# Value-times-output product of a cross-attention kernel: keys on the output partitions, 26 of 154 tokens in four 32-column float32 tiles ahead of a 128-token main product

## Chip, cores and metric

One core of one Trainium2 chip. The metric is device microseconds (us) of one execution, lower is better.

## What is computed

`x` is 2 x 2048 x 512 (queries), `ctx_768` is 2 x 77 x 384 (keys and values), 8 heads of width 512:

```python
Q = (img_embed @ Wq).reshape(B, -1, H, D).transpose(0, 2, 1, 3)
K = (sent_embed @ Wk).reshape(B, -1, H, D).transpose(0, 2, 1, 3)
V = (sent_embed @ Wv).reshape(B, -1, H, D).transpose(0, 2, 1, 3)
score = jnp.einsum('bhqd,bhkd->bhqk', Q, K) / math.sqrt(D)
attn = softmax(where(mask, score, -inf))
ctx = jnp.einsum('bhqk,bhkd->bqhd', attn, V).reshape(B, -1, H * D)
out = ctx @ Wo + img_embed
return (out - mean) * rsqrt(var + 1e-5) * gamma + beta
```

Everything is float32. The two products with the queries are reassociated: A = Wq K^T and VW = V Wo are made per head from the 154 tokens (2 batches x 77 keys), so that the queries meet only A (scores) and VW (output).

## The kernel before

**Two stages.** The first is a loop over 16 uses `u` (8 key heads, then 8 value heads, `H` = 8). The second goes over 32 tiles of 128 queries, in 16 pairs `p`: seven block products with A (a Strassen-like scheme), softmax, a transpose of the probabilities, and the product with VW, then the layer norm.

**Numbers in two parts.** Most products are made of float32r parts: a rounded `hi` and a remainder `lo`, three terms out of four. `short_product` (L538) takes hi weights against a moving operand that holds hi and lo side by side (304 or 308 columns), and lo weights against hi alone (152 or 154). `full_product` (L546) multiplies plain float32; each float32 matmul of the code is two records of 154 columns in the trace.

**A use u.** TensorE (PE) makes `project(u+1)` or `project_full(u+1)` (tokens times Wk or Wv, 12 matmuls of the code), and then the out product of `u` (16 matmuls of the code: `out_product` or `out_product_full`). Weights stand still, so the tokens are the columns of the result and the model dimension is on its partitions. ACT rounds the weights (`round_w_proj` L828, `round_w_out` L836), the projected values (`round_kv` L846), and takes the out product (L853). GpSimd (POOL) makes the `lo` part of the projection weights (L1489), VectorE (DVE) the `lo` part of the out weights (`split_w_out`, L1061), of the projected values (`split_kv`, L1080 to L1089) and of A (L1105 to L1113). Which value heads go in parts and which in plain float32 is set by hand (`SPLIT_VALUES`, `FULL_VALUES`): projections of 8, 9, 13, 14, 15 and out products of 8, 12, 13, 14 are in parts.

**VW.** The out product of a value head lies as model x tokens in `vw_t`. The second stage wants keys on the partitions, so `transpose_vw` (L651) turns blocks of 128 rows over TensorE inside the out products of uses 10, 12, 13, 15 and once more in `first_products(0)`: 40 transposes of 128 columns. ACT (L861) and DVE (L1130) split each into `vw_hi` and `vw_lo`: 10 instructions of 512 columns each.

**The T sums.** During uses 8 to 10 DVE also makes the sums that the block scheme needs: `right_sum` (L1159, 16 instructions of 608 columns, both inputs in SBUF), `split_t` (L1164, 8 of 608 columns); ACT rounds them (`round_t`, L900). They read all of A, so they start after the last key head.

**Order.** Each engine runs its own list in program order; semaphores connect them. In use 8 and later DVE has, in this order: `split_kv(u+1)` (or `add_kv`), `split_vw`, and behind them the T sums of that use. `project_full(u+1)` starts by waiting for what DVE or ACT made of the projection of `u` (`wait_kv(u)`), because it overwrites the same PSUM banks. The DMA queue of SyncE (SP) loads weights in rings of three, then the query blocks.

**Start of the second stage.** `bias_rows` (L1144) waits for the out product of use 14, ACT's `seed(0)` (L871) waits for it, `first_products(0)` waits for the seed. In DVE's list `split_vw(H, [0])` stands between `add_u2(0)` (L1177) and `add_w2(0)` (L1182), and the product S4 in `last_products(0)` waits for `add_w2(0)`. `normalise` (L1243, L1246) scales 616 probabilities by the reciprocal of their sums before `transpose_prob` (L724); `out_rows` (L737) is 15 matmuls of 512 columns.

Of the kernel before, what the change touches and what calls it, by code (L numbers as in the profile page):

```python
# [26 lines left out]
F32 = mybir.dt.float32  # L27
F32R = mybir.dt.float32r
# [10 lines left out]
PAD_FROM = 96  # L39


class Shapes:


    def __init__(self, x_tiles, ctx_t, w_proj, w_out, mask):
# [15 lines left out]
        self.slot = self.keys + self.keys % 2  # L61
        self.key_t = -(-self.row // P)
        self.per_batch = self.tiles // self.batches
        assert self.toks == self.batches * self.keys and self.half <= BANK and self.heads % 2 == 0
        assert 2 * self.toks <= BANK and self.model <= BANK and self.dim_t == self.model_t == 4
        assert self.batches == 2 and self.kept % 2 == 0 and self.heads // 2 * self.slot <= BANK

    def key_rows(self, j):
        return min(P, self.row - j * P)


def transposes_during(s):


    plan, j = [], 0
    for h in range(s.heads + 1):
        ready = []
        while j < s.key_t and j * P + s.key_rows(j) <= s.keys * h:
            ready += [(j, b) for b in range(s.batches)]
            j += 1  # L80
        plan.append(ready)
    return plan


def build(nc, x_tiles, x_rows, ctx_t, wk, wq_t, wv, wo, mask, gamma, beta, out):
# [8 lines left out]
    SPLIT_VALUES = (H, *range(H + 4, USES - 1))  # L94
    FULL_VALUES = (H + 2, H + 3, H + 4)
# [10 lines left out]
    plan = transposes_during(s)  # L106
    groups = [g for part in plan for g in part]
    group_no = {g: n for n, g in enumerate(groups)}

    with ExitStack() as stack:  # L110
# [47 lines left out]
        with ExitStack() as values:  # L158
            v_t0 = values.enter_context(nc.sbuf_tensor("v_t0", [P, s.dim_t, s.toks], F32))
            values.enter_context(nc.sbuf_tensor("gap6", [P, s.dim_t, s.toks], F32))  # L160
            v_t = [v_t0, values.enter_context(nc.sbuf_tensor("v_t1", [P, s.dim_t, s.toks], F32))]
# [4 lines left out]
        with ExitStack() as spare:  # L166
            t_tmp4 = [spare.enter_context(nc.sbuf_tensor(f"t_tmp4_{n}", [P, KT, s.kept_half], F32)) for n in range(3)]
# [5 lines left out]
        w_proj_hi = []  # L173

        def vw_and_proj(name, n):

            with ExitStack() as early:
                early.enter_context(nc.sbuf_tensor(f"vw_first{n}", [P, FREE_VW, s.batches, s.model], F32R))
                w_proj_hi.append(early.enter_context(nc.sbuf_tensor(f"w_proj_hi{n}", [P, s.dim_t, s.ctx_t, P], F32R)))
            return sb(name, [P, s.key_t, s.batches, s.model], F32R)  # L180
# [18 lines left out]
        sb("gap2", [P, 288])  # L199
# [1367 lines left out]
```

## Time and profile before

| | us |
|---|---|
| median of 3 runs | 352.82 (352.49 to 353.0) |
| the profiled execution, its own time | 353.7 |
| its span in the profile | 351.9 |
| PE busy | 346.0 (98%), 2272 matmuls |
| DVE busy | 288.0 (82%) |
| ACT busy | 243.7 (69%) |
| POOL busy | 213.3 (61%) |
| PE clock granted | 9 tenths or more in every one of 40 slices |

The profiled execution's time is its span and 1.8 us around it. A busy share counts time in which an instruction of the engine is under way; matmuls overlap, so the start of one to the start of the next is what one costs.

### The profile page before, as it was taken

To read this page: it belongs to the slowest core of one execution; us is meant where nothing else is said; L and a number is where in the kernel's file an instruction comes from. 1 tells how busy PE (TensorE), PEld (TensorE's weight loads), DVE (VectorE), ACT (ScalarE), POOL (GpSimd) and SP (SyncE) were. 2 spreads that over 40 slices of the span, in tenths; PEclk is the share of its full clock that TensorE was granted. 3 is DMA by queue.
4 is the path that set the end of the run, shared out by engine and by line. 5 is a ranking of instruction groups with operands and counts; after the bars stand their busy time and mean duration, and the time that the engine had idled before them with its cause. 6 is when DMAs were issued, how large, how long until landed. Compare 5 with 4: busy or idle time off the path is not lost. (4 is left out here: it accounts for less than half of the span.)

```text
span 351.9 us, 6894 instructions
## 1 busy us (share of the span) xinstructions
PE 346.0 (98%) x2272; PEld 322.0 (92%) x2272; DVE 288.0 (82%) x532; ACT 243.7 (69%) x797; POOL 213.3 (61%) x218
## 2 busy tenths in 40 slices
PE   9999999999999999999999999999999999999994
PEld 6999999999999999998899899889988998899884
DVE  2149999999778768898797988988987989889896
ACT  2268766645777669887886976968778769768560
POOL 0044654400447968689769688687796796885243
PEclk9999999999999999999999999999999999999999
DMA  7998769775635080053142341440532423413012
GB/s 229 423 420 323 280 223 324 281 276 218 221 137 212 0 275 29 1 179 113 68 171 75 116 151 59 152 151 31 181 95 85 152 72 138 149 41 111 32 44 107
DMA packets 19683, 55.81 MB, mean 159 GB/s; under 512 B 1728, under 2 KB 3264, under 8 KB 17728
## 3 DMA queue, kind: packets, MB, share of 16 engines
q1 hardware_dynamic: 18784, 54.38, 42.6%
q10 hardware_dynamic: 864, 1.00, 0.8%
q8 instruction: 18, 0.29, 0.4%
q14 instruction: 17, 0.14, 0.1%
HBM read 46.98 MB, written 8.39 MB: 157 GB/s over the span
## 5 line engine op out<-in xcount | busy, mean ns | idle before, releaser
L1489 POOL TENSOR_TENSOR w_proj_lo<-w_proj,w_proj_hi 128x768 fp32r<-128x768 f32 x20 | 36.9, 1868 | 73.1 <-ACT w_proj_hi L828 73.1
L737 PE MATMUL pair<-vw_hi,pt_hi 128*128 128x512 f32 x155 | 62.1, 400 | 0.0
L737 PE MATMUL pair<-vw_lo,pt_hi 128*128 128x512 f32 x155 | 60.9, 393 | 0.0
L737 PE MATMUL pair<-vw_hi,pt_lo 128*128 128x512 f32 x155 | 60.7, 392 | 0.0
L1438 POOL TENSOR_TENSOR out_sb<-centred,beta_sb 128x512 f32<-128x512 f32 x30 | 38.8, 1295 | 28.8 <-ACT centred L939 28.7
L894 ACT ACTIVATE prob<-c,neg_max 128x77 f32<-128x77 f32 x128 | 43.9, 347 | 0.0
L1483 POOL TENSOR_TENSOR xo_lo<-x_sum,xo_hi 128x512 fp32r<-128x512 f32 x32 | 41.5, 1301 | 0.2 <-ACT xo_hi L918 0.2
L538 PE MATMUL pair<-kv_t,w_out_hi 128*128 128x304 f32 (+1 forms) x160 | 41.6, 334 | 0.0
L661 PE MATMUL pair<-a_hi,xo_hi 128*128 128x304 f32 x128 | 40.0, 313 | 0.0
L661 PE MATMUL pair<-a_lo,xo_hi 128*128 128x304 f32 x128 | 38.6, 302 | 0.0
L661 PE MATMUL pair<-a_hi,xo_lo 128*128 128x304 f32 x128 | 38.6, 301 | 0.0
L1262 DVE TENSOR_TENSOR pair<-pair,x_in 128x512 f32<-128x512 f32 x31 | 21.7, 699 | 19.5 <-PE pair L737 19.3
L932 ACT ACTIVATE pt_hi<-pair 128x640 fp32r<-128x640 f32 x32 | 22.5, 704 | 21.4 <-PE pair L724 21.4
L1061 DVE TENSOR_TENSOR w_out_lo<-w_out,w_out_hi 128x1024 fp32r<-128x1024 f32 x20 | 33.1, 1692 | 3.8 <-ACT w_out_hi L836 3.7
L885 ACT ACTIVATE prob<-pair,neg_max 128x77 f32<-128x77 f32 x64 | 19.9, 325 | 23.0 <-DVE neg_max L1205 23.0
L737 PEld LDWEIGHTS pair<-vw_hi,pt_lo 128*128 128x128 f32 x155 | 29.2, 188 | 6.3
L737 PEld LDWEIGHTS pair<-vw_hi,pt_hi 128*128 128x128 f32 x155 | 29.2, 188 | 5.4
L737 PEld LDWEIGHTS pair<-vw_lo,pt_hi 128*128 128x128 f32 x155 | 29.2, 188 | 5.0
L1477 POOL TENSOR_TENSOR xo_lo<-xt_in,xo_hi 128x512 fp32r<-128x512 f32 (+1 forms) x32 | 33.2, 1038 | 0.9 <-ACT xo_hi L911 0.9
L1432 POOL TENSOR_TENSOR rstd<-var_eps,minus_half 128x1 f32<-128x1 f32 x32 | 17.7, 553 | 25.5 <-DVE var_eps L1283 25.5
L538 PE MATMUL pair<-kv_t,w_out_lo 128*128 128x152 f32 (+1 forms) x160 | 32.5, 244 | 0.0
L661 PE MATMUL pair<-t_hi,xo_hi 128*128 128x304 f32 x96 | 29.5, 307 | 0.2 <-DVE c L1201 0.2
(129 smaller groups left out, 1022.3 us busy)
## 6 DMA issues: line engine op xcount, KB each, us to landing
w_out<-wo SPq DMA_DIRECT2D x8, 1024.0 KB, 4.8
xt_in<-x_tiles SPq DMA_DIRECT2D x16, 512.0 KB, 4.0
x_in<-x_rows SPq DMA_DIRECT2D x16, 512.0 KB, 4.7
out<-out_sb SPq DMA_DIRECT2D x31, 256.0 KB, 2.1
w_out<-wq_t SPq DMA_DIRECT2D x7, 1024.0 KB, 8.1
w_proj<-wv SPq DMA_DIRECT2D x8, 768.0 KB, 4.7
w_proj<-wk SPq DMA_DIRECT2D x6, 768.0 KB, 9.9
w_out<-wq_t SPq DMA_DIRECT2D x2, 512.0 KB, 8.2
```

Of the source, the lines that this page charges most:

```text
L538: mm = pe.matmul(pair[:, bank, 0:n], w[:, m, k, :], moving[:, k, 0:n], start=(at == 0), stop=(at == len(steps) - 1))
L661: mm = pe.matmul(bank, xs[:, left, k, :], kept_heads(r[:, k, :]), start=(begin and k == 0 and n == 0), stop=(k == KT - 1 and n == len(pass ...
L737: mm = pe.matmul(ps_out[:, i % 2, 0:s.model], ps[:, j, :], v[:, j, b, :], start=(j == 0 and n == 0), stop=(j == s.key_t - 1 and n == len(p ...
L885: e = act.activation(prob[i % 2][:, h * s.keys:(h + 1) * s.keys], src, ACT.Exp, bias=neg_max[i % 2][:, h:h + 1], accum_out=sums[i % 2][:, ...
L894: e = act.activation(prob[i % 2][:, cols], c2[:, cols], ACT.Exp, bias=neg_max[i % 2][:, h:h + 1], accum_out=sums[i % 2][:, h:h + 1])
L932: act.activation(pt_hi[i % 2][:, :, :], pt_blocks, ACT.Copy).then_inc(act_pt_hi, 1)
L1061: dve.tensor_tensor(half_cols(w_out_lo[u % W_RING], half), half_cols(w_out_sb[u % W_RING], half), half_cols(w_out_hi[u % 2], half).bitcast ...
L1262: dve.tensor_tensor(y, ps_out[:, i % 2, 0:s.model], x_in[c % X_RING][:, i % CHUNK, :], ALU.add)\
L1438: pool.tensor_tensor(out_sb[i % OUT_RING][:, :], centred[i % 2][:, :], beta_sb[:, :], ALU.add)\
L1477: pool.tensor_tensor(xo_lo[p % 2][:, blocks, :, :], src, xo_hi[p % 2][:, blocks, :, :].bitcast(F32), ALU.subtract).then_inc(pool_xo_lo, 1)
L1483: pool.tensor_tensor(xo_lo[p % 2][:, blocks, :, :], x_sum[:, at:at + 2, :, :], xo_hi[p % 2][:, blocks, :, :].bitcast(F32), ALU.subtract).t ...
L1489: pool.tensor_tensor(half_cols(w_proj_lo[u % W_RING], half), half_cols(w_proj_sb[u % W_RING], half), half_cols(w_proj_hi[u % 2], half).bit ...
```

## The change

VW is made with the tokens on the output partitions: the projected values stand still, the rows of Wo move (512 columns). Of the 154 tokens, 128 in the middle (the last 64 keys of one batch and the first 64 of the other) are the main product in three float32r passes, 12 matmuls of 512 columns. The 26 others (13 at each end) are padded to 32 (`v_rest`) and multiplied in plain float32, in four column tiles of the array, one for each 128 columns of Wo: 16 matmuls of the code with 128 moving columns. They write 32 partitions each; ACT copies them to `strip_sb`, and SP moves each in 8 small DMAs to `rest_rows`, from which the fifth block of VW is split at the start of the second stage. Odd heads take the tokens with the batches exchanged (`ctx_turned`). The transposes and `vw_t` go. All value heads are projected in plain float32, all out products are in parts; the `lo` weights of uses 8 to 13 are made by POOL, those of 14 and 15 by DVE. `normalise` writes the 13 end keys of each head to `prob_rest` with an instruction of its own.

```diff
-    SPLIT_VALUES = (H, *range(H + 4, USES - 1))
-    FULL_VALUES = (H + 2, H + 3, H + 4)
+    RESTS_OF_VECTOR = (USES - 2, USES - 1)
+    STRIPS = P // STRIP
...
         def whole(u):
-            return u < FULL_PROJ or u in FULL_VALUES
+            return u < FULL_PROJ or u >= H
         def whole_out(u):
-            return u < FULL_OUT or (u >= H and u not in SPLIT_VALUES)
+            return u < FULL_OUT
+        def by_vector(u):
+            return u < H or u in RESTS_OF_VECTOR
...
+            def move_strips(h):
+                sp.wait_ge(act_strip, h + 1)
+                for g in range(STRIPS):
+                    for n in range(s.batches):
+                        b = (h + n) % 2
+                        to, at = place(h, b) * s.rest, g * STRIP + n * s.rest
+                        sp.dma_start(rest_rows[to:to + s.rest, b, g * P:(g + 1) * P],
+                                     strip_sb[h % 2][at:at + s.rest, :]).then_inc(ld_rest[h % 2], DMA_INC)
...
                 load_w_out(u)
+                if u >= H + W_RING:
+                    move_strips(u - H - W_RING)
             for c in range(XT_RING):
                 load_xt(c)
+            for h in range(H - W_RING, H):
+                move_strips(h)
...
+            def value_product(u):
+                h = u - H
+                hi, lo = wide(w_out_hi[u % 2]), wide(values_lo(u))
+                wait_kv(u, 1)
+                if u == USES - 1:
+                    open_bank_a()
+                if h == 0:
+                    pe.wait_ge(dve_a_lo, 2 * H)
+                elif h >= 2:
+                    pe.wait_ge(dve_vw_lo, 2 * (h - 1))
+                for k in range(s.dim_t):
+                    if k % 2 == 0:
+                        pe.wait_ge(act_o_hi, 2 * split_before(u) + k // 2 + 1)
+                        pe.wait_ge(dve_o_lo if by_vector(u) else pool_o_lo,
+                                   rests_before(u, by_vector(u)) + k // 2 + 1)
+                    passes = [(0, hi), (0, lo), (1, hi)]
+                    for n, (low, w) in enumerate(passes):
+                        mm = pe.matmul(ps_vw[h % 2], values(u, k, low), w[:, k, :], start=(k == 0 and n == 0),
+                                       stop=(k == s.dim_t - 1 and n == len(passes) - 1))
+                mm.then_inc(pe_outp, 1)
+            def value_strips(u):
+                h, w = u - H, wide(w_out_sb[u % W_RING])
+                pe.wait_ge(pool_v_rest, h + 1)
...
+                for k in range(s.dim_t):
+                    for g in range(STRIPS):
+                        mm = pe.matmul(ps_strips[h % 2][g * STRIP:(g + 1) * STRIP, :], v_rest[u % 2][:, k, :],
+                                       w[:, k, g * P:(g + 1) * P], start=(k == 0), stop=(k == s.dim_t - 1))
+                mm.then_inc(pe_outp, 1)
...
                 if whole_out(u):
                     out_product_full(u)
+                elif u < H:
+                    out_product(u)
                 else:
-                    out_product(u)
+                    value_strips(u)
+                    value_product(u)
...
+            def take_strips(h):
+                act.wait_ge(pe_outp, 2 * (H + h) + 1)
...
+                act.activation(strip_sb[h % 2][:, :], ps_strips[h % 2], ACT.Copy).then_inc(act_strip, 1)
+            def split_rest():
+                for n in range(2):
+                    act.wait_ge(ld_rest[n], DMA_INC * STRIPS * s.batches * (H // 2))
...
             for u in range(USES):
+                if u + 1 < USES and u >= H:
+                    round_w_out(u + 1)
                 if u + 1 < USES:
                     round_kv(u + 1)
...
                 if u == USES - 1:
                     seed(0)
-                if u >= H:
-                    split_vw(u - H)
...
+                take_strips(u - H)
+                split_vw(u - H)
...
             copy_s1(0)
             round_sums(1)
-            split_vw(H)
+            split_rest()
             exps_first(0)
...
                 if u + 1 < USES and not whole_out(u + 1):
                     split_kv(u + 1)
-                elif u + 1 < USES and summed_kv(u + 1):
-                    add_kv(u + 1)
                 if u == H:
                     right_sum(T1, 0)
...
+                if u + 1 < USES and by_vector(u + 1):
+                    split_w_out(u + 1)
...
             add_u2(0)
-            split_vw(H, [0])
+            split_rest(0)
             add_w2(0)
...
+            for u in range(H, USES):
+                if not by_vector(u):
+                    for half in range(2):
+                        pool.wait_ge(act_o_hi, 2 * split_before(u) + half + 1)
+                        pool.tensor_tensor(half_cols(values_lo(u), half), half_cols(w_out_sb[u % W_RING], half),
+                                           half_cols(w_out_hi[u % 2], half).bitcast(F32), ALU.subtract)\
+                            .then_inc(pool_o_lo, 1)
+                pool.wait_ge(dve_kv_lo, 2 * split_before(u) + 2)
...
+                pool.tensor_tensor(v_rest[u % 2][:, :, 0:s.rest_toks].rearrange("p m (n k) -> p m n k", n=2),
+                                   rest_values(u, 0), rest_values(u, 1), ALU.add)\
+                    .then_inc(pool_v_rest, 1)
+                if u == USES - 2:
+                    block_sums(0)
```

`values(u, k, low)` is the 128 tokens from column 13 on of `kv_t[u % 2]`, its hi or its lo part; `wide(w)` is a row block of Wo as 512 columns. `ctx_turned` is copied by POOL at the start of the kernel, while POOL has nothing else.

## Rows read from the trace of the kernel before

**Rows 1.** Busy time in stretches (us, then PE, PEld, DVE, ACT, POOL, clock, DMA).

```profile
65.48:68.52 3.04, 3.04 (x26) 3.04 (x26) 3.04 (x2) 1.24 (x3) 1.11 (x1) 1.00 0.54 175
68.52:72.55 4.03, 4.03 (x34) 4.03 (x33) 3.93 (x8) 0.86 (x2) 0.00 (x0) 1.00 0.84 324
72.55:75.69 3.14, 3.14 (x25) 3.14 (x25) 3.07 (x6) 0.86 (x2) 0.00 (x0) 1.00 0.54 179
75.69:79.89 4.20, 4.20 (x34) 4.20 (x33) 4.03 (x6) 2.85 (x5) 0.00 (x0) 1.00 0.81 309
98.50:103.40 4.90, 4.90 (x41) 4.90 (x41) 2.88 (x8) 3.58 (x7) 3.46 (x2) 1.00 0.26 109
140.00:340.00 200.00, 199.80 (x1182) 180.11 (x1181) 172.56 (x350) 153.76 (x609) 147.62 (x163) 1.00 0.29 104
```

**Rows 2.** Timeline of PE (start us, us): output product, stage two's start, its S4, kernel's start.

```profile
151.54 0.39 PE L737 MATMUL pair<-vw_hi,pt_hi 128*128 128x512 f32 x1
151.77 0.39 PE L737 MATMUL pair<-vw_lo,pt_hi 128*128 128x512 f32 x1
...
123.52 0.41 PE L661 MATMUL pair<-a_hi,xo_hi 128*128 128x304 f32 x1
...
128.68 0.30 PE L661 MATMUL pair<-a_hi,xo_hi 128*128 128x304 f32 x1
...
0.77 3.57 PE L759 MATMUL pair<-const-bfloat16-1.0 128*128 128x512 bf16 x8 [0.77 <-PEq L1560]
```

**Rows 3.** POOL by tile (duration ns min/median/max) and its timeline at use 13.

```profile
L1489 POOL TENSOR_TENSOR w_proj_lo<-w_proj,w_proj_hi x20: 1818/1861/2062, 21.0 to 109.7; 128x768 fp32r<-128x768 f32 x20
...
L1483 POOL TENSOR_TENSOR xo_lo<-x_sum,xo_hi x4: 1276/1282/1289, 117.6 to 126.9; 128x512 fp32r<-128x512 f32 x4
...
92.70 3.64 POOL L1489 TENSOR_TENSOR w_proj_lo<-w_proj,w_proj_hi 128x768 fp32r<-128x768 f32 x2 [26.11 <-ACT w_proj_hi L828]
```

**Rows 4.** Timeline and tiles where DVE and POOL both read two SBUF tensors.

```profile
57.68 1.86 POOL L1489 TENSOR_TENSOR w_proj_lo<-w_proj,w_proj_hi 128x768 fp32r<-128x768 f32 x1
58.19 2.44 DVE L1061 TENSOR_TENSOR w_out_lo<-w_out,w_out_hi 128x1024 fp32r<-128x1024 f32 x1
...
112.17 1.23 DVE L1061 TENSOR_TENSOR w_out_lo<-w_out,w_out_hi 128x1024 fp32r<-128x1024 f32 x1 [0.15 <-ACT w_out_hi L836]
112.33 1.69 POOL L1460 TENSOR_TENSOR x_sum<-x_sum,xt_in 128x256 f32<-128x256 f32 x1
113.31 1.78 DVE L1061 TENSOR_TENSOR w_out_lo<-w_out,w_out_hi 128x1024 fp32r<-128x1024 f32 x1
...
L1460 POOL TENSOR_TENSOR x_sum<-x_sum,xt_in x2: 734/1210/1685, 112.3 to 122.1; 128x256 f32<-128x256 f32 x2
```

**Rows 5.** Timeline of DVE, T sums and their remainders.

```profile
78.55 2.44 DVE L1159 TENSOR_TENSOR t_tmp<-t_tmp,t_tmp 128x608 f32<-128x608 f32 x3
...
83.72 1.49 DVE L1164 TENSOR_TENSOR a_lo<-t_tmp,a_hi 128x608 fp32r<-128x608 f32 x2
```

**Rows 6.** Timeline of ACT, rounding of out weights and of VW.

```profile
63.98 2.00 ACT L836 ACTIVATE w_out_hi<-w_out 128x1024 fp32r<-128x1024 f32 x2
...
122.34 1.08 ACT L861 ACTIVATE vw_hi<-pair 128x512 fp32r<-128x512 f32 x2 [0.41 <-PE pair L651]
```

**Rows 7.** Timelines of DVE and SP around the second stage's start; DMA issues (KB, us to landing).

```profile
119.55 1.85 DVE L1144 TENSOR_TENSOR mask_bias<-mask_low 128x308 f32<-128x308 f32 x2
...
126.64 0.69 DVE L1130 TENSOR_TENSOR vw_lo<-pair,vw_hi 104x512 fp32r<-104x512 f32 x1 [0.67 <-ACT vw_hi L861]
127.25 0.46 DVE L1182 TENSOR_TENSOR u_w<-pair,u_w 128x304 f32<-128x304 f32 x1
...
123.82 1.39 SPq L467 DMA_DIRECT2D x_in<-x_rows  x3
...
out<-out_sb SPq DMA_DIRECT2D x1, 128.0 KB, 1.7
```

**Rows 8.** DVE by tile: scaling of the probabilities (duration ns min/median/max).

```profile
L1246 DVE TENSOR_TENSOR prob<-prob,pair x32: 795/796/797, 132.7 to 337.5; 128x616 f32<-128x616 f32 x32
```

More of the change, by code:

```diff
@@ L39 @@
 PAD_FROM = 96
+STRIP = 32
 class Shapes:
@@ L61, in __init__ @@
         self.slot = self.keys + self.keys % 2
+        self.main = P // self.batches
+        self.rest = self.keys - self.main
+        self.rest_toks = self.batches * self.rest
+        self.rest_rows = self.heads * self.rest
         self.key_t = -(-self.row // P)
@@ L65, in __init__ @@
         assert 2 * self.toks <= BANK and self.model <= BANK and self.dim_t == self.model_t == 4
+        assert 0 < self.rest_toks <= STRIP and self.rest_rows <= P and self.heads * self.main == (self.key_t - 1) * P
         assert self.batches == 2 and self.kept % 2 == 0 and self.heads // 2 * self.slot <= BANK
[L68 to L82, printed above, removed]
 def build(nc, x_tiles, x_rows, ctx_t, wk, wq_t, wv, wo, mask, gamma, beta, out):
@@ L340, in head_cols @@
         def head_cols(t, half, h):
-            keys = s.kept if t is a_hi or t is a_lo else s.keys
-            return t[:, 2 * half:2 * half + 2, :, h * keys:(h + 1) * keys]
+            rows = t[:, 2 * half:2 * half + 2, :, h * s.kept:(h + 1) * s.kept]
+            apart = s.kept_row + (place(h, 1) - h) * s.kept
+            return bass.AP(rows.tensor, rows.offset, [*rows.ap[0:2], [apart, s.batches], rows.ap[-1]])
         def tile_cols(w, m):
@@ L384, in split_before, with rests_before, values, ends_of @@
             return sum(not whole_out(v) for v in range(u))
-        def summed_before(u):
-            return 2 * sum(not whole_out(v) for v in range(H, u))
-        def value_of(u):
-            return kv_full[u] if u < FULL_OUT else v_t[u % 2][:, :, :]
+        def rests_before(u, of_vector):
+            return 2 * sum(not whole_out(v) and by_vector(v) == of_vector for v in range(u))
+        def by_vector(u):
+            return u < H or u in RESTS_OF_VECTOR
+        def values(u, k, low):
+            at = low * s.toks + s.rest
+            return kv_t[u % 2][:, k, at:at + P]
+        def ends_of(rows, count):
+            return bass.AP(rows.tensor, rows.offset,
+                           [*rows.ap[:-1], [2 * s.keys, count], [2 * s.keys - s.rest, 2], [1, s.rest]])
+        def rest_values(u, low):
+            return ends_of(kv_t[u % 2][:, :, low * s.toks:(low + 1) * s.toks], 1)[:, :, 0, :, :].bitcast(F32)
+        def mains_of(t):
+            return t.rearrange("p (j k) -> p j k", k=2 * s.keys)[:, :, s.rest:s.rest + P]
+        def place(h, b):
+            return h ^ b
+        def values_lo(u):
+            return wo_lo_even if (u - H) % 2 == 0 else wo_lo_odd[1] if u < H + 5 else wo_lo_late
+        def vw_half(v, h, n):
+            return v[n * s.main:(n + 1) * s.main, h // 2, (n + h) % 2, :]
+        def wide(w):
+            return w[:, :, :, :].rearrange("p k m c -> p k (m c)")
         def nth_product(p, n):
```

243 lines of the change are left out of this document (105 added, 138 removed).

## The prediction

> **What bounds the kernel now.** I read the table of stretches first. In each stretch of the value heads PE is busy for all of it, at full clock, and from 140 to 340 us it works 199.80 of 200 us [rows 1]. The view of waits names PE for nothing but the 0.77 us at the very start [rows 2]. So PE bounds both stages, and each microsecond added to its list or put as a gap into it is lost. DVE is busy 172.56 of 200 us in the second stage [rows 1]. In the value heads it is nearly as full as PE (3.93 of 4.03 us, 3.07 of 3.14), while POOL is empty there: before 92.70 it sat idle for 26.11 us [rows 3]. The second view is the timeline where DVE and POOL work together. A DVE subtraction of 1024 columns from two SBUF tensors takes 1.23 us alone, but 2.44 us when it begins at 58.19, with a POOL instruction under way until 57.68 + 1.86 = 59.54: 59.54 + 1.2 is when it ended. The other way round, POOL's 0.73 us sum began at 112.33 and took 1.69, for it had to let the DVE instruction of 112.17 end; and the next one of DVE (1.78) waited for that [rows 4]. So where both engines read two SBUF tensors they go one at a time, a whole instruction each, in turn.
>
> **PE's own work, use 8 to the end of 15.** Removed: four out products in parts at 4.03 and four plain ones at 4.20, 32.9 us, and 32 transposes of four calls at 4.90 - 4.03 = 0.87 each, 3.5 us (the fifth call is after the end of use 15) [rows 1]. Together 36.4. Added: per head a main product of 12 matmuls of 512 columns, which start 151.77 - 151.54 = 0.23 us apart [rows 2], so 2.74 us; and the strips. Projections: five go from 3.04 to 3.14 [rows 1], +0.5.
>
> The strips are the first unknown. A plain projection is 24 records of 154 columns in 3.14 us, 0.131 us each [rows 1]; at 128 columns that is 0.109. A head has 16 strip matmuls, 32 records. If nothing overlaps that is 3.5 us; if four tiles run at once, 0.9. The two records of one matmul need the same columns of the array one after the other, and the neighbour's first can only run beside the second of them if starts keep their order. That is half of the serial price, and between the two ends: I take 2.0 us with a little for starts. Then a head costs 4.74 and eight cost 37.9: PE's work grows by 37.9 - 36.4 + 0.5 = 2.0 us.
>
> The Trainium skill (TensorE: Matmul & The Clock Gate, Part 3, packing of small matmuls) measured 2.38 times the speed for three column tiles; carried over to four that would make a head's strips about 1.1 us (an estimate), and PE's work would shrink by 5 us instead. It speaks of matmuls of one pass, and no run here shows column tiles.
>
> **Gap 1, before the strips of use 8: 1.7 us.** The strips wait for `v_rest`, which stands in POOL's list behind both halves of `w_out_lo(8)`. ACT rounds those at 63.98 and gives the first free at 65.0 [rows 6]. POOL's price for 1024 columns isn't in the trace: 768 take 1.86, 512 take 1.28 [rows 3], so 2.4. Two halves from 65.1 end at 69.9, the small sum at 70.4 (0.45, an estimate below the 0.73 of 256 columns [rows 4]). PE has done the projection of 9 at 68.7. Lower bound 0 (if POOL could start at the landing), upper 2.5.
>
> **Gap 2, before the projection of 11: 7.7 us.** Before, the projected values of 10 needed ACT alone; now `project_full(11)` waits for DVE's `split_kv(10)`, which stands behind nine T sums. PE: strips from 70.5, product of 8 done at 75.2, projection of 10 78.4, strips 80.4, product of 9 83.1; here it wants `kv(10)`. DVE: `split_vw(0)` can start at 75.9 (ACT 0.5 [rows 6]), but in front of it T1's three sums alternate with POOL's `w_out_lo(9)` (70.4 on), so it ends at 79.4. Then nine sums at 2.44 / 3 = 0.81 [rows 5], 7.4 us, and between them POOL's two halves of `w_out_lo(10)`, of which 3.6 us fall into this piece, since DVE and POOL take turns [rows 4]. 79.4 + 11.0 + 0.4 = 90.8. Without the turns it would be about 1.9 us.
>
> **Gap 3, before the projection of 12: 5.0 us.** PE needs 3.15 + 2.0 + 2.74 = 7.9 us for the next three pieces. DVE needs from 90.8: the other half of `kv(10)` 0.4, two splits of VW 1.2, six `split_t` at 0.72 [rows 5] 4.3, POOL's two halves of `w_out_lo(11)` between them 4.8, two sums 1.6, `kv(11)` 0.4: 12.8. Without POOL's turns 8.0, a gap of 0.1. Then PE does the projection, strips and product of 11 by 111.6, and four heads with three projections, 4 x 4.74 + 3 x 3.15 = 28.4, end at 140.0 against 123.52 [rows 2]. That is 16.5 later. In these last heads ACT has some 4.5 us and POOL 5.3 to do in 7.9: no gap.
>
> **Gap 4, before S4 of the first pair: net 3.4 us.** Before, S4 began 5.16 us after use 15's end [rows 2]. Now a chain of small DMAs is ahead of it. `bias_rows` (1.85 [rows 7], and two turns of POOL, 1.5) waits for the product of 14, which now ends only 4.7 us before the end; the seed follows at +0.7 to +1.1 and holds ACT's `take_strips(7)`; SP issues eight DMAs at 1.39 / 3 = 0.46 or somewhat less [rows 7], to +4.9; the last lands 1.7 to 2 later, by the smallest DMA of the trace [rows 7], +6.8; ACT 0.5, DVE 0.6, `add_w2` 0.4 [rows 7]: S4 at +8.5. Bounds: 0 if the DMAs are issued and land in half that, 5 if they meet others. Behind it the fifth transposition call is gone, already counted in the 5.16.
>
> **At nothing.** `normalise` pays 0.80 us for 616 columns [rows 8]; 512 and 104 apart cost perhaps 0.15 more, 32 times on DVE, which has 27 of 200 us idle [rows 1], and PE reads the result some 4 us later. Cover gone, it would be 4.8 us in all, at worst. The five pairs of weight roundings that go from ACT, the four out-weight subtractions that go from DVE, and the early copies on POOL lie beside PE's work. SP's 64 small DMAs take 3.4 us per head in a queue where a load is issued about one head ahead of its use; bounds 0 and 2 us.
>
> **Clock.** All stretches show full clock [rows 1]; but the first eight matmuls after nothing took 3.57 / 8 = 0.45 us for 512 columns instead of 0.23 [rows 2], the 1.2 GHz level. Gaps of 5 to 8 us could bring that back. The price of one restart from these rows is 1.7 us; gaps 3 and 4 could each leave one, so 0 to 3.4, and I take 1.4.
>
> The Trainium skill (TensorE: Matmul & The Clock Gate, Part 1) says that an idle array falls back to half its clock; no gap of this trace is long enough to show it.
>
> **Sum.** 2.0 + 1.7 + 7.7 + 5.0 + 3.4 + 1.4 = 21.2 us. The profiled execution took 353.7 (span 351.9 and 1.8), so it would show 374.9, a span of 373.1; the median of the runs is 0.9 lower, so 374.0.
>
> **The rivals.**
> *Turns harmless (0.17).* POOL's work falls where DVE uses PSUM inputs or waits. Gaps 2 and 3 are 1.9 and 0.1, the sum 2.0 + 1.7 + 2.0 + 3.4 = 9.1: 362; with strips at 1.1 us, 7 less from PE but some back in the gaps, about 356. For it: splits with a PSUM input aren't slowed. Against: T sums are SBUF only and fill DVE's list here.
> *Strips serial (0.12).* 3.5 us, eight times 1.5 more, of which gaps 2 and 3 take back 6: 380. For it: every record has its own weight load, and in the trace a load goes with each matmul.
> *Faster: four tiles at once (0.13).* One mechanism, at the strips: 0.9 us per head. PE's work falls by 36.4 - 29.1 - 0.5 = 6.8 us, and the fifth transposition call (0.8) with it; if the four gaps together stay under 7.6 us the kernel is faster, and with none of them it is 352.8 - 7.6 = 345.2. It decides from 1.75 us per head on. Against it: each gap is a wait in program order and is longer when PE arrives sooner.
> *No difference (0.03)*, where these cancel within 0.2%, about 0.7 us, which is what a measurement of this kernel can tell from nothing.
> The forecast has 0.55. That the change doesn't do what it says (tiles placed apart) is the serial case.
>
> **Numbers.** 374.0. With serial strips and a restart 381, without turns 356: these two ends leave out the faster cases and little else. Slower: 0.55 + 0.17 + 0.12 = 0.84.
>
> **What would show it.** Right: PE idle before the first record of the projections of uses 11 and 12, put down to DVE `kv_t`; DVE's T sums taking 2 to 3.2 us each when POOL's 1024-column instruction is under way; PE idle before the first strips (POOL `v_rest`) and before S4; the second stage as long as before. Wrong: strips of about 1 us and PE without idle time in the value heads, or T sums that stay at 0.8 us beside POOL. If 16 strip matmuls take other than 2.0 us, the first term fails and the rest stands.

## The result, and the profile after

The changed kernel takes 374.90 us (median of 4 runs, 373.82 to 375.72), the kernel before on the same chip 352.91 (4 runs, 352.49 to 353.11): a ratio of 1.0623 with a 95% interval of 1.059 to 1.0656, 22.0 us slower. The profiled execution below took 375.72 with a span of 373.9, which is 22.0 more than the span before.

The page of the kernel after: the span, the busy time of each engine, and of the 40 slices of the span the busy tenths of PE and DVE and the clock granted to PE.

```profile
span 373.9 us, 7129 instructions
PE 346.6 (93%) x2328; PEld 313.7 (84%) x2328; DVE 295.3 (79%) x557; ACT 245.0 (66%) x794; POOL 231.1 (62%) x232
PE   8999999793699963999999999999999999999994
DVE  2269997679972782789898898889888889889896
PEclk9999999896999997899999999999999999999998
```

PE is busy for 346.6 us, the same to 1 us as before, but 93% of the span instead of nearly all of it. The lost time is in slices 8 to 16, from 70 to 150 us. The next view is PE's timeline there: start, duration, line, operation, number of records, and in brackets the idle time ahead of it and what ended it. The rows without brackets show one undisturbed head.

```profile
70.56 1.85 PE L693 MATMUL pair<-w_out,v_rest 128*32 128x128 f32 x32 [1.97 <-POOL v_rest L1539]
90.48 5.40 PE L586 MATMUL pair<-ctx_turned,w_proj 128*128 128x154 f32 x24 [7.11 <-DVE kv_t L1126]
102.90 3.38 PE L586 MATMUL pair<-ctx_sb,w_proj 128*128 128x154 f32 x24 [3.02 <-DVE kv_t L1126]
113.39 1.08 PE L693 MATMUL pair<-w_out,v_rest 128*32 128x128 f32 x32
117.29 3.31 PE L586 MATMUL pair<-ctx_sb,w_proj 128*128 128x154 f32 x24
120.53 1.08 PE L693 MATMUL pair<-w_out,v_rest 128*32 128x128 f32 x32
133.34 1.08 PE L693 MATMUL pair<-w_out,v_rest 128*32 128x128 f32 x32 [1.61 <-POOL v_rest L1539]
139.20 0.38 PE L703 MATMUL pair<-a_hi,xo_hi 128*128 128x304 f32 x1 [1.76 <-ACT pair L921]
149.30 0.62 PE L703 MATMUL pair<-a_hi,xo_hi 128*128 128x304 f32 x1 [5.72 <-DVE u_w L1216]
```

Before, PE was busy in all of each stretch of the value heads [rows 1]. Now there are six gaps, 21.2 us in all: before the strips of use 8, before the projections of uses 11 and 12, before the strips of 15, before the first pair's product behind the seed, and before its S4. A head that nothing holds takes 7.14 us (113.39 to 120.53): 1.01 for the strips, 2.89 for the main product, 3.24 for the projection.

Why `kv_t` came late is seen where DVE's T sums (L1193) meet POOL's low weights (L1533). DVE and POOL, timeline:

```profile
71.19 2.83 DVE L1193 TENSOR_TENSOR t_tmp<-t_tmp,a_lo 128x608 f32<-128x608 f32 x1
78.29 0.79 DVE L1193 TENSOR_TENSOR t_tmp<-a_hi,a_lo 128x608 f32<-128x608 f32 x1
79.12 2.87 DVE L1193 TENSOR_TENSOR t_tmp<-t_tmp,a_hi 128x608 f32<-128x608 f32 x1
82.02 2.85 DVE L1193 TENSOR_TENSOR t_tmp<-t_tmp,a_lo 128x608 f32<-128x608 f32 x1
78.60 5.62 POOL L1533 TENSOR_TENSOR wo_lo_even<-w_out,w_out_hi 128x1024 fp32r<-128x1024 f32 x2 [1.97 <-ACT w_out_hi L874]
107.87 4.73 POOL L1533 TENSOR_TENSOR wo_lo_even<-w_out,w_out_hi 128x1024 fp32r<-128x1024 f32 x2 [4.27 <-ACT w_out_hi L874]
```

A T sum is 0.79 us. Each one that meets POOL's pair of 1024 columns is 2.8 to 2.9, 2.0 to 2.1 longer: it waits out nearly a whole POOL instruction (4.73 / 2 = 2.37 undisturbed). POOL's pair grows from 4.73 to 5.62, by about one T sum. These are the turns of [rows 4], with larger instructions. The two held sums at 79 and 82 us are 4.1 of the 7.11 us of the gap before the projection of 11; the other 3.0 are DVE's own list in front of `kv_t` (an estimate, from these rows). The sum held at 71.19 cost nothing, since DVE then waited 2.83 us for ACT, until 76.85.

The tail, from the timelines of SP's queue, ACT and DVE:

```profile
76.60 6.45 SPq L527 DMA_DIRECT2D rest_rows<-strip_sb  x8
117.48 0.34 SPq L519 DMA_DIRECT2D w_out<-wo  x1
117.87 6.69 SPq L527 DMA_DIRECT2D rest_rows<-strip_sb  x8
124.69 0.94 SPq L488 DMA_DIRECT2D xt_in<-x_tiles  x2
125.69 20.65 SPq L527 DMA_DIRECT2D rest_rows<-strip_sb  x24
147.51 1.15 ACT L911 ACTIVATE vw_hi<-rest_rows 104x512 fp32r<-104x512 f32 x2 [5.72 <-DMA rest_rows<-strip_sb]
148.17 0.69 DVE L1163 TENSOR_TENSOR vw_lo<-rest_rows,vw_hi 104x512 fp32r<-104x512 f32 x1 [6.57 <-ACT vw_hi L911]
```

One small DMA keeps SP's queue for 0.8 us (6.45 / 8), and the last 24, which the kernel puts behind the loads of x transposed (`xt_in`), stand one behind the other until 146.34. ACT waits 5.72 us for the last of them, DVE 6.57 for ACT, PE's S4 5.72 for DVE.

Last, stretches of the kernel after: length, busy time and number of instructions of PE, PEld, DVE, ACT and POOL, then PE's granted clock, DMA share and GB/s.

```profile
70.50:76.10 5.60, 5.54 (x45) 4.44 (x46) 3.49 (x2) 0.28 (x1) 5.60 (x3) 0.70 0.26 103
90.40:95.90 5.50, 5.42 (x28) 5.29 (x32) 5.44 (x6) 3.43 (x5) 3.75 (x3) 0.62 0.04 9
102.80:106.30 3.50, 3.40 (x28) 3.27 (x32) 3.40 (x6) 0.35 (x2) 0.38 (x1) 1.00 0.42 161
113.30:120.50 7.20, 7.20 (x70) 6.25 (x68) 2.24 (x4) 4.27 (x8) 4.66 (x3) 1.00 0.45 155
149.30:152.30 3.00, 3.00 (x12) 3.00 (x13) 1.81 (x6) 1.76 (x9) 0.00 (x0) 0.50 1.04 375
```

Behind the gaps of 1.97, 7.11 and 5.72 us the granted clock is 0.70, 0.62 and 0.50 on average, which is wholly or partly the level of 1.2 GHz; behind that of 3.02 it is 1.00.

### The profile page after: what moved, and what is told of

The parts are those of the page before. It is cut to its first block and busy times, and to the rows that moved or that the text cites. A ratio compares the mean times of both kernels' runs of the same rounds, so it can differ in the third digit from the quotient of the medians.

```text
span 373.9 us, 7129 instructions
## 1 busy us (share of the span) xinstructions
PE 346.6 (93%) x2328; PEld 313.7 (84%) x2328; DVE 295.3 (79%) x557; ACT 245.0 (66%) x794; POOL 231.1 (62%) x232
## 5 line engine op out<-in xcount | busy, mean ns | idle before, releaser
L1526 POOL TENSOR_TENSOR w_proj_lo<-w_proj,w_proj_hi 128x768 fp32r<-128x768 f32 x10 | 18.4, 1862 | 28.3 <-ACT w_proj_hi L866 28.3
L703 PEld LDWEIGHTS pair<-a_hi,xo_hi 128*128 128x128 f32 x128 | 24.5, 191 | 8.7 <-DVE u_w L1216 6.0
L703 PE MATMUL pair<-t_lo,xo_hi 128*128 128x304 f32 x96 | 29.3, 305 | 0.0
L703 PE MATMUL pair<-t_hi,xo_lo 128*128 128x304 f32 x96 | 29.2, 305 | 0.0
```

Of the source, the lines that this page charges most:

```text
L703: mm = pe.matmul(bank, xs[:, left, k, :], kept_heads(r[:, k, :]), start=(begin and k == 0 and n == 0), stop=(k == KT - 1 and n == len(pass ...
L1526: pool.tensor_tensor(half_cols(w_proj_lo[u % W_RING], half), half_cols(w_proj_sb[u % W_RING], half), half_cols(w_proj_hi[u % 2], half).bit ...
```

## The experiments

The theory: DVE and POOL take turns where both read two SBUF tensors, and that makes `kv_t` of uses 10 and 11 late; a second, separate delay comes from the strips' small DMAs in the tail. Rivals: DVE has too much to do even without turns; the strips on PE are what costs. Each run below is beside runs of the kernel before on the same chip.

### Low weights on DVE alone

```diff
-    RESTS_OF_VECTOR = (USES - 2, USES - 1)
+    RESTS_OF_VECTOR = range(H, USES)
```

> All eight value heads' low weights are made by DVE instead of POOL for six of them; nothing else changes. Theory (DVE and POOL take turns on two-input SBUF instructions): DVE gets 2.3 us more per head, but none of its T sums is held, all take 0.8 us; the gap before the strips of use 8 goes, the one before the projection of 11 falls from 7.1 to about 4, that of 12 stays near 3, and the kernel gains 5 to 7 us, to about 369. Rival (only the order of DVE's list makes the gaps, turns cost nothing): DVE's list in front of split_kv(10) and (11) grows by 2.3 us each, the gaps grow, 375 or more.

371.76 us, ratio 1.0538 (1.052 to 1.0556). PE's timeline of this kernel before the projection of 11:

```profile
83.25 6.17 PE L586 MATMUL pair<-ctx_turned,w_proj 128*128 128x154 f32 x24 [3.94 <-DVE kv_t L1126]
```

And DVE's T sums, those that took 2.87 and 2.85 us in the changed kernel:

```profile
76.02 0.79 DVE L1193 TENSOR_TENSOR t_tmp<-t_tmp,a_hi 128x608 f32<-128x608 f32 x1
76.84 0.79 DVE L1193 TENSOR_TENSOR t_tmp<-t_tmp,a_lo 128x608 f32<-128x608 f32 x1
```

The gap is 3.94 instead of 7.11, though DVE has four more pieces of 1.23 to make before it, two of them behind its first T sums. The gap before the strips of use 8 is gone. The gap before 12 fell from 3.02 to 0.38, and a new one of 2.00 stands before 13, where DVE is now too full. So the turns were real, and giving the work to DVE trades them for load. The gap of 3.94 us was followed by the slow clock (0.54 over the 6.2 us): the projection took 6.10 us from its start to the next piece, where it took 5.33 in the changed kernel and takes 3.24 undisturbed.

### Strips tile by tile

```diff
-                for k in range(s.dim_t):
-                    for g in range(STRIPS):
+                for g in range(STRIPS):
+                    for k in range(s.dim_t):
```

> The two loops of the strips are exchanged, so that the four matmuls of one column tile follow each other before the next tile. Theory (a strip costs 1.0 us because neighbours in the list are on different tiles and run together): consecutive records meet the same columns, strips go to about 3.5 us per head, 20 us more for eight, of which the two gaps in the T sums take back about 5: about 390. Rival (0.03 us per record is what an instruction costs to issue, whatever tile it has): strips stay at 1.0 us and the time at 375.

382.30 us, ratio 1.081 (1.078 to 1.0839). Two records from its PE timeline:

```profile
123.13 3.31 PE L586 MATMUL pair<-ctx_sb,w_proj 128*128 128x154 f32 x24
126.37 2.46 PE L693 MATMUL pair<-w_out,v_rest 128*32 128x128 f32 x32
```

From the start of one projection to the start of the next are 8.51 us (131.64 - 123.13), less 3.24 and 2.89: 2.4 for the strips, against 1.0 when neighbours in the list are of different tiles. Not the serial 3.5 either. Eight heads times 1.38 are 11.0 us. The gaps before projections 11 and 12 (5.76 and 2.17 here), before the strips of 15 (none), at the seed (0.21) and before S4 (4.78) took back 6.3, and the slow clock, by what is then left, took 1.9 more than in the changed kernel (the projection of 12 in 5.05 instead of 3.38, the first strips 4.05, the projection of 11 4.85). That makes 6.6; the spans differ by 6.5 (380.4 and 373.9). The strips' price in the changed kernel, 1.0 us, is thereby settled, and so is that it is low because neighbours in the list are of different tiles: the rival, 0.03 us as the price of an issue whatever the tile, would have left the time at 375.

### The tail's order and the early `v_rest`

The rows' rounding on ACT and DVE moved behind the first probabilities, the first loads of x transposed issued at use 14, `v_rest(8)` ahead of POOL's low weights of 8.

```diff
+                if u == USES - 2:
+                    for c in range(XT_RING):
+                        load_xt(c)
...
-            split_rest()
             exps_first(0)
             copy_s1(1)
             exps_second(0)
+            split_rest()
```

> Three moves: ACT's and DVE's split of rest_rows goes behind the first softmax, the two loads of query blocks go ahead of the strips' small DMAs of uses 11 and later, and POOL takes v_rest(8) ahead of its low weights of use 8. Theory (these lists hold PE): the 5.7 us gap before S4 and the slow clock behind it (1.4) go, the 1.6 us one before the strips of use 15 and the 2.0 before those of use 8 go with its slow clock (1.6); about 364. Rival (another wait stands behind each: the small DMAs' landing itself, or DVE's list): at most 3 us are won, 372 or more.

372.56 us, ratio 1.0539 (1.0512 to 1.0567), a miss: 2.3 us gained where 11 were expected, as the rival had it. The gaps before the strips of 8 and 15 and before S4 are gone, but the time went elsewhere: 0.62 before the strips of 9, the one before projection 11 grew to 8.19, the seed's to 2.43, and 4.0 us appeared in the main loop (1.91 behind `vw_lo`, 0.91, 1.21). For the 1.91 us behind `vw_lo` PE waited for the same late rows, further down its list. Before projection 11 DVE's T sums were held as before, four of them to 1.88 to 2.88 us each.

### A quarter of the low weights

```diff
+                        part = slice(0, 1) if u in (H + 2, H + 3) else slice(0, s.model_t)
```

with `[:, :, part, :]` on POOL's three operands. It leaves out three quarters of the low parts of `wo` for uses 10 and 11.

> POOL makes only a quarter of the low weights of uses 10 and 11 (256 columns instead of 1024 in each of four instructions); the other three quarters are left out, so these two heads use stale low weights. DVE's list and its work are untouched. Theory (turns): the DVE sums held by POOL take 1.5 us each instead of 2.9, the gap before the projection of 11 falls from 7.1 to about 3.8, that of 12 from 3.0 to about 0, in all 6 us: 369. Rival (order alone): no change, 375.

369.97 us, ratio 1.0461 (1.0417 to 1.0506). PE and DVE of this kernel:

```profile
85.01 5.05 PE L586 MATMUL pair<-ctx_turned,w_proj 128*128 128x154 f32 x24 [3.81 <-DVE kv_t L1126]
76.94 1.21 DVE L1193 TENSOR_TENSOR t_tmp<-t_tmp,a_hi 128x608 f32<-128x608 f32 x1
78.18 1.22 DVE L1193 TENSOR_TENSOR t_tmp<-t_tmp,a_lo 128x608 f32<-128x608 f32 x1
```

The same two T sums that took 2.87 and 2.85 take 1.21 and 1.22 when POOL's instruction has a quarter of the columns. What they wait beyond their own 0.79 us falls from 2.07 to 0.42, as POOL's instruction falls from 1024 to 256 columns, which is what turns of whole instructions mean. The gap before projection 11 falls by 3.30, as much as the two sums are shorter (3.29); 3.81 are left, nearly all of it DVE's own list. The gap before projection 12 is gone, the others unchanged. The profiled execution took 367.31 us and is 2.7 below the median; the clock accounts for part of that, as the last section shows.

### Three heads in plain float32

Uses 9 to 11: `v_t` as a float32 copy, the main product from `w_out_sb` and `v_t` in four float32 matmuls of 512 columns, no roundings and no low weights.

```diff
+                if u in PLAIN:
+                    for k in range(s.dim_t):
+                        at = plain_values(u)[:, k, s.rest:s.rest + P]
+                        mm = pe.matmul(ps_vw[h % 2], at, wide(w_out_sb[u % W_RING])[:, k, :], start=(k == 0),
+                                       stop=(k == s.dim_t - 1))
+                    mm.then_inc(pe_outp, 1)
+                    return
```

> Uses 9, 10 and 11 (value heads 1 to 3) are made in plain float32: no high and low parts of their weights or values, four float32 matmuls of 512 columns per head for the main product, and v_rest copied instead of summed. The four passes of float32 over 512 columns should take 3.6 us where the twelve products take 2.89 (2.1 us more in three heads). Theory of the turns (POOL's low weights against DVE's T sums and kv_t): the gaps of 7.11 us before the projection of use 11 and 3.02 before that of 12 vanish, and with them the slow projection behind the first (5.33 instead of 3.24): 374.9 - 7.1 - 3.0 - 2.1 + 2.1 = 365 us, range 362 to 368. The gap of 1.97 before the strips of use 8 and those of the tail (1.6, 1.8, 5.7) stay. Rival (the T sums and splits of DVE are too much work even undisturbed, so that kv_t comes late without any turn): a gap of 3 to 4 us stays before the projection of 11 and the time is 369 or more. Rival (values without their low parts change nothing, since the release comes from elsewhere): 375.

366.79 us, ratio 1.0383 (1.0349 to 1.0418). PE's timeline:

```profile
85.24 1.08 PE L709 MATMUL pair<-w_out,v_rest 128*32 128x128 f32 x32
86.25 3.70 PE L683 MATMUL pair<-w_out,v_t 128*128 128x512 f32 x8
98.13 2.07 PE L595 MATMUL pair<-ctx_turned,w_proj 128*128 128x154 f32 x14 [0.39 <-DVE kv_t L1142]
```

The gaps before the projections of 11 and 12 are gone, and so is the slow clock behind the first; a new one of 0.39 us stands before that of 13 (the last row); the plain product costs 3.54 (86.25 to the projection at 89.79), 0.65 more than the twelve. The time is 8.1 us below the changed kernel, within the range told. The gaps at both ends stay: 2.50 before the strips of 8 and 2.23 before those of 15, both a little longer, 1.75 and 5.71 around S4.

### The same with the tail mended

As above, with `v_rest(8)` first, the early loads of x transposed, `mask_bias` made at use 12 in the memory of the T sums, and the rows split batch by batch.

```diff
-                if u == USES - 1:
+                if u == H + 4:
                     bias_rows()
...
             split_pt(0)
+            split_rest([0])
...
+                    if j == s.key_t - 1 and i % s.per_batch == 0:
+                        pe.wait_ge(dve_vw_lo, 2 * H + b + 1)
```

> As e4_plain, and with the tail mended as well: POOL makes v_rest(8) before the low weights of use 9; the first load of x transposed is issued at use 14, ahead of the strips' small DMAs; bias rows are made at use 12 in the memory of the T sums instead of at use 15; the strips' rows are split batch by batch, the first after the transposed probabilities of tile 0, the second after those of tile 1. If the gaps found at both ends (1.97 before the strips of 8; 1.61, 1.76 and 5.72 around S4, 1.4 of slow clock behind it) come from those causes, and the two groups (turns, tail) add up: 365 - 2.0 - 0.8 - 9 - 1.4 = 352 us, range 349 to 358, level with the kernel before at 353. Rival (the waits of the tail only move, as in e3_tail, where 4 us of the gaps came back inside the main loop): 357 to 361.

360.73 us, ratio 1.0209 (1.017 to 1.0248). No gap over 0.3 us but 0.39 up to the main loop, and then 6.2 us in it. SP and ACT of this kernel:

```profile
104.72 26.68 SPq L538 DMA_DIRECT2D rest_rows<-strip_sb  x32
131.45 1.55 SPq L505 DMA_DIRECT2D x_in<-x_rows  x3
133.11 0.93 SPq L499 DMA_DIRECT2D xt_in<-x_tiles  x2
139.87 0.63 ACT L981 ACTIVATE xo_hi<-xt_in 128x512 fp32r<-128x512 f32 x1 [5.55 <-DMA xt_in<-x_tiles]
```

The rival had it right: 32 strip DMAs in a row hold the queue until 131.4, the loads of x come behind them, and the tail's wait has moved to x. 6.1 us came off where 13 were expected.

### And with the low weights on DVE

`RESTS_OF_VECTOR = range(H, USES)` on top of it.

> As e6_plain_tail, with the low weights of uses 12 and 13 (and of 8) made by DVE instead of POOL, so that POOL and DVE hold one another nowhere in the value heads. DVE has 4 x 1.23 us more to do in two heads of 7.1. If the turns still cost something in uses 12 and 13: 1 to 2 us below e6_plain_tail. If DVE is then too full, a gap before the projection of 13 or 14 of 2 us and 1 to 3 us above it. My forecast: within 1.5 us of e6_plain_tail.

358.50 us, ratio 1.0155 (1.014 to 1.017): 2.2 below the last, a little beyond the forecast. With three heads plain, DVE has the room that it lacked in the first experiment. But nothing came off the value heads: from the strips of 8 to those of 15 PE needs 49.4 us in both kernels (68.27 to 117.69 and 67.88 to 117.28). 0.9 of the 2.2 us is a shorter wait for x in the main loop (5.25 instead of 6.18), where SP's row of 32 strip DMAs takes 25.61 us instead of 26.68; why it does is not shown.

### All heads plain

`PLAIN = range(H + 1, USES)` on top of the mended tail.

> As e6_plain_tail, with all of uses 9 to 15 in plain float32: no low weights behind use 8, so no turns at all, and ACT and DVE with some 20 us less work each. PE pays 0.7 us per head in four more heads: 352 + 2.8 = 355 us if e6_plain_tail has no gaps left in uses 12 to 15; level with it or faster if it has over 3 us of gaps there. Rival (the float32 product costs no more than the twelve, as both read the same columns): 350.

359.75 us, ratio 1.0191 (1.0152 to 1.023). No wait over 0.5 us up to the main loop, and the same wait for x (6.4 us, before a product of the second pair) stands in it. So by then neither DVE nor POOL nor the turns set the time: SP's queue does.

### The loads of x ahead of the last strips, and two plain heads instead of three

```diff
-            for h in range(H - W_RING, H):
+            for h in range(H - W_RING, H - 1):
                 move_strips(h)
             sp.wait_ge(pe_outp, 2 * USES)
             for c in range(X_RING):
                 load_x(c)
+            move_strips(H - 1)
```

> As e7_plain_tail_dve (358.5 us), with SP issuing the three loads of x rows ahead of the last head's eight strip DMAs instead of behind them. In e7_plain_tail_dve the strips' issues keep SP from 104.8 to 129.6 us; the x rows go out at 129.62, the third load of x transposed at 131.41, and ACT waits 4.63 us for it until 138.54, behind which PE stands idle 5.2 us. Theory (the small DMAs' issues on SP delay the loads, and the load of x transposed is slow because the x rows go out just ahead of it): the load still goes out at 131.4 but lands by 134, the wait of PE falls from 5.2 to 1 us or less, and the time is 354 to 355 us. Rival (the load takes 7 us whatever is beside it, or the strips' last DMAs become what PE waits for): 358 or more.

356.63 us, ratio 1.0101 (1.0086 to 1.0116), the nearest to the kernel before, and between forecast and rival. PE's idle time there:

```profile
141.79 0.41 PE L723 MATMUL pair<-a_hi,xo_hi 128*128 128x304 f32 x1 [2.79 <-ACT pair L942]
```

2.79 instead of 5.2, not under 1: the load of x transposed was issued at 133.10, later than thought, since the eight issues are only shifted. It was there 3.3 us later, at 136.38, and not 7.1 us as behind the x rows; that part of the theory held. Behind the wait the clock fell once more:

```profile
143.07 0.46 PE L723 MATMUL pair<-t_hi,xo_hi 128*128 128x304 f32 x1
```

From 142.31 to 145.60 such products start 0.25 us apart instead of 0.14, which costs some 1.5 us.

> As e9_x_first, with two value heads (uses 9 and 10) in plain float32 instead of three. Each plain head costs PE about 0.7 us; but in use 11 DVE then has the low weights (2.5 us) and the second half of kv_t (0.95) to do again beside the splits of T4. If DVE has that slack: 0.7 us faster than e9_x_first. If not: a gap of 1 to 3 us before the projection of use 12 or 13, and as much slower. My forecast: 1 us slower.

`PLAIN = (H + 1, H + 2)` gave 360.58 us, ratio 1.0214 (1.0191 to 1.0237). Slower by 4 us, not by 1: waits of 1.92 before projection 12 and 1.99 before that of 13, both for DVE's `kv_t`.

```profile
90.15 3.38 PE L599 MATMUL pair<-ctx_sb,w_proj 128*128 128x154 f32 x24 [1.92 <-DVE kv_t L1148]
```

DVE's slack in these heads is under one head's low weights.

### Half of the last strips issued by ACT

Base: the kernel with the low weights on DVE.

```diff
-                for g in range(STRIPS):
+                for g in range(STRIPS if h < H - W_RING else STRIPS // 2):
...
+            def move_half(h):
+                act.wait_ge(act_strip, h + 1)
+                for g in range(STRIPS // 2, STRIPS):
+                    for n in range(s.batches):
...
+                        act.dma_start(rest_rows[to:to + s.rest, b, g * P:(g + 1) * P],
```

> As e7_plain_tail_dve (358.5 us), with half of the strip DMAs of the last three heads issued by ACT instead of SP, so that SP has 12 issues of 0.8 us fewer in front of the loads of x. Theory (SP's issues are the bound of the tail): x rows go out at about 122 us, as soon as the last main product is done, the third load of x transposed when its buffer is free, 129; the wait of PE in the second pair goes: 353 to 354 us, level with the kernel before or faster than e9_x_first. Rival (an issue costs ACT the same 0.8 us, and ACT's splits of the weights and copies of the head then come late): 358 to 362.

357.48 us, ratio 1.0132 (1.0114 to 1.0151). ACT's queue and ACT itself:

```profile
120.46 2.51 ACTq L932 DMA_DIRECT2D rest_rows<-strip_sb  x3
123.06 0.63 ACT L990 ACTIVATE xo_hi<-xt_in 128x512 fp32r<-128x512 f32 x1 [2.37 <-issue]
```

An issue costs ACT the same 0.8 us, and ACT does nothing else meanwhile (2.37 us of "issue"). PE's wait for x (5.25) is gone: the load goes out 1.8 us earlier, and PE comes later, by new waits for ACT (0.99, 1.07) and POOL (1.82) in its timeline. The median is 1.0 us better than without, the intervals of the two ratios overlap, and the time lies between forecast and rival: the price is mostly moved.

### Strips ahead of the out weights' load

```diff
+                if u >= H + W_RING:
+                    move_strips(u - H - W_RING, range(0, 2))
                 load_w_out(u)
...
-                    move_strips(u - H - W_RING)
+                    move_strips(u - H - W_RING, range(2, STRIPS))
```

> As e9_x_first (356.6 us), with the first four of each head's eight strip DMAs issued ahead of the load of out weights of the same turn, which waits for the end of that head's main product, 2.9 us behind the strips. SP, which issues without a pause from 104.7 to 133 us in e9_x_first, then starts that row some 2.9 us earlier. Theory (SP's time for issues is what the loads of x wait for): x rows go out at 122 to 123 instead of 125.1, the third load of x transposed at 130 instead of 133.1, the wait of PE in the second pair falls from 2.8 to under 1 us, and the time is 353.8 to 355 us. Rival (the load's landing or something else sets it): 356 or more. A load of out weights that now goes out late would show as PE idle before a main product and cost 1 to 2 us.

357.85 us, ratio 1.0116 (1.0096 to 1.0137), a miss; no better than the kernel with the loads first, as the rival had it. SP's queue:

```profile
109.35 0.35 SPq L530 DMA_DIRECT2D w_out<-wo  x1
109.76 15.75 SPq L538 DMA_DIRECT2D rest_rows<-strip_sb  x20
125.55 1.54 SPq L505 DMA_DIRECT2D x_in<-x_rows  x3
```

The last load of out weights slipped from 104.15 to 109.35, and the x rows still went out at 125.5. A head's eight issues (6.3 us) and two loads (0.5 each) are 7.3 us on SP, and a head is 7.1 to 7.8 us on PE: the queue is full, and an order can't make room in it. This is what the two misses of the tail have in common.

## Why the prediction was right, and where it wasn't

The forecast was 374.0 and 374.9 came; the sum of the six terms was 21.2, and 22.0 was lost. But this agreement is luck: it is made of errors that cancel. Against their terms PE's own work came out 5.6 us lower, gap 1 0.3 higher, gap 2 0.6 and gap 3 2.0 lower, a gap in no term 1.6 higher, gap 4 3.5 higher and the clock 3.7 higher, together 0.9.

**PE's own work: forecast +2.0, measured -3.6.** Product 15 ends at 137.27 instead of 123.52 [rows 2], 13.75 later; gaps ahead of it are 1.97 + 7.11 + 3.02 + 1.61 = 13.71, and the slow clock behind two of them took 3.7 (strips and main product of 8: 5.47 instead of 3.90; projection of 11: 5.33 instead of 3.24). What is left is -3.6. The step that failed is "that is half of the serial price, and between the two ends: I take 2.0 us": neighbouring float32 matmuls of different tiles overlap nearly fully, 32 records in 1.01 us, 0.03 each, and only the order tile by tile costs 2.4. That alone is 8 x 0.99 = 7.9 us. The main product was 2.89 instead of 2.74 and a projection in this surrounding 3.24 instead of 3.14, which took back some 2 us. The estimate worked out from the Trainium skill (TensorE: Matmul & The Clock Gate, Part 3), 1.1 us per head, was the better one, and the measured 1.01 lies close to it. That page gives its figure for three tiles and names no number format.

**Gap 1: forecast 1.7, measured 1.97.** POOL's pair took 4.68, as the step had it, and `v_rest` 0.94 beside a T sum instead of 0.45; undisturbed ones take 0.38.

**Gap 2: forecast 7.7, measured 7.11. Gap 3: forecast 5.0, measured 3.02.** Mechanism and place as told: `kv_t` behind T sums that alternate with POOL. Two experiments that took the turns away or shortened them without touching the waits (DVE alone; a quarter of the columns) took 3.2 and 3.3 us from gap 2 and nearly all of gap 3, and the plain heads took both. The single T sum is held for 2.05 us, a POOL instruction less 0.3. But the share of the turns in gap 2 was forecast as 5.8 of 7.7 and was 4.1 of 7.11; DVE's own list makes 3.0 of it, not 1.9. PE came to gap 2 at 83.37, the time of the forecast (83.1): what the short strips save was lost to the slow clock, the main products and the projection. Gap 3 is shorter because PE needed 9.4 us for the three pieces before it instead of 7.9 (its projection ran on the slow clock), with DVE at 12.4 instead of 12.8. By this arithmetic 2.1 of the 3.7 us of slow clock below lie in time that PE would have waited anyway. The rival "turns harmless" falls by the 2.87 us sums.

**Gap 4: forecast net 3.4, measured 6.9.** S4 stands 12.03 us behind product 15 instead of 5.16. The seed's wait (1.76) and the DMAs' (5.72) are both there. The mis-sized term is "eight DMAs at 1.39 / 3 = 0.46": an SBUF to SBUF DMA of 13 rows costs SP 0.8, and not 8 but 24 of them stood in the queue, the last three heads', which the kernel puts behind the loads of x transposed. Here "at nothing ... bounds 0 and 2 us" failed too: 64 issues at 0.8 take 51 us of SP. The first load of x transposed went out at 124.69 instead of 104.04. Before, it came straight behind the last load of out weights, whose issue ended at 103.92; now that load is issued until 117.82, 13.9 us later, since it waits for the product of 12, which ends at 117.29, and eight strip DMAs, 6.7 us, stand behind it. Before, SP's queue, and after, POOL's timeline:

```profile
104.04 0.89 SPq L461 DMA_DIRECT2D xt_in<-x_tiles  x2
128.01 0.75 POOL L1488 TENSOR_TENSOR x_sum<-xt_in 128x256 f32<-128x256 f32 x1 [4.56 <-DMA xt_in<-x_tiles]
132.91 0.38 POOL L1539 TENSOR_TENSOR v_rest<-kv_t 128x104 f32<-128x104 f32 x1
```

POOL makes its sums of x ahead of `v_rest` of 15, so these came late and with them the strips of 15. This is the wait of 1.61, in no term; where the load goes out earlier (the mended tail) it is gone.

**Clock: forecast 1.4, measured 3.7 ahead of product 15 and some 1.4 behind S4.** The price of a restart was right in kind; there were three instead of one. The Trainium skill (TensorE: Matmul & The Clock Gate, Part 1) says that an idle array falls back to half its clock; the granted 0.50 behind S4's wait agrees. The 1.00 behind the gap of 3.02 shows that not every gap does it.

**The rest.** The main loop is as long as before but for that 1.4. "Faster: four tiles at once" had its mechanism right (0.9 predicted for its condition, 1.01 measured) and its result wrong, by its own "against": the gaps came to 21 us and not under 7.6. Taking them out one by one led to 356.63, still 1% over the kernel before. In that kernel product 15 ends 1.9 us earlier than before, at 121.64, with three plain heads at +0.65 in it, so PE does save; but from there to the end it needs 233.2 us instead of 228.4. Of these 4.8 us, 3.6 are waits (2.79 for the load of x, the others under 0.4 each) and some 1.5 the slow clock behind that wait, while the fifth transposition call (0.8) is gone; 0.5 is not explained. Fewer or larger DMAs for the strips were not tried: the destination rows change their batch every 13 partitions, and a way to cover them with fewer was not found.

## What to carry to other kernels

A shorter list for the busiest engine is worth what its next waits leave of it: before moving work off PE, lay out when each input of the next pieces is ready if PE comes earlier. Where VectorE and GpSimd both read two SBUF tensors, price each meeting at one whole instruction of the other engine, and keep GpSimd's instructions short beside a chain that PE waits for. Count small DMAs by their issues, at 0.8 us of a queue each, and see what load stands behind them.

## What the runs showed of the hardware

- Float32 matmuls of 128x32 tiles, 32 records: 1.01 us when neighbours in the list are different tiles, 2.4 us when the four matmuls of a tile follow one another. Same work, same data.
- A T sum of 608 columns: 0.79 us alone, 2.83 to 2.87 beside POOL instructions of 1024 columns, 1.21 beside those of 256.
- An SBUF to SBUF DMA of 13 rows of 512 bytes: 0.74 us at best on SP's queue, 0.77 on ACT's, where the engine stands still for it.
- The granted clock after a gap is not a matter of the gap alone. After 1.97 us of waiting for `v_rest` the strips ran in 1.85 us in the kernel after (granted 0.70 over the stretch) and in 1.08 in the quarter kernel (1.00), behind a gap of the same 1.97; behind 2.17 us (strips tile by tile) the projection of 12 took 5.05 us, behind 3.02 in the kernel after the usual 3.38; behind the gaps of 3.81, 3.94, 5.72 and 7.11 it was low each time. Behind 2.79 (loads of x first) it fell half a microsecond into the next products, behind 2.00 (DVE alone) and 2.72 (the tail's order) it did not. The runs of one kernel with gaps over 3 us spread over 1.0 to 3.5 us, those of the kernel before over 0.6 to 0.9. The clock goes with it: of the quarter kernel's four runs those of 367.31 and 369.14 us had a mean granted clock of 0.986 and 0.984, those of 370.80 and 370.85 of 0.975. What decides it is open.
